# Causal mask of the second attention scores: added by TensorE instead of cut by GpSimd, with the exponentials taken twice from PSUM

## What is computed

```python
x = x + 0.5 * ffn(layernorm(x))      # silu(x Wg) * (x Wu), times Wd; hidden width 2048
x = x + attention(layernorm(x))      # 16 heads of 32
x = x + 0.5 * ffn(layernorm(x))

q, k = unit_norm(q), unit_norm(k)    # then rotary embedding on every other head
logits = einsum('bshd,bthd->bhst', q, k) * q_gain
logits = where(causal, logits, finfo.min)
attn   = softmax(logits, axis=-1)
y      = einsum('bhst,bthd->bshd', attn, v)
```

## Time and profile before

| | |
|---|---|
| profiled execution | 2897.56 us |
| its span | 2895.8 us |
| TensorE (PE) busy | 2765.8 us, 96% |
| VectorE (DVE) busy | 1773.8 us, 61% |
| ScalarE (ACT) busy | 1193.0 us, 41% |
| GpSimd (POOL) busy | 535.8 us, 19% |

### The profile page before, as it was taken

One profiled execution on the slowest core, in us unless ns is written; L12 is line 12 of the kernel. 1 busy time (PEld: TensorE's weight loads), 2 busy tenths in 40 slices (PEclk: granted clock), 3 DMA queues, 4 the chain that ended last, 5 costly groups with the idle time before them and its releaser, 6 DMA issues.

```text
span 2895.8 us, 56172 instructions
## 1 busy us (share of the span) xinstructions
PE 2765.8 (96%) x23232; PEld 2029.6 (70%) x23232; DVE 1773.8 (61%) x4156; ACT 1193.0 (41%) x2218; POOL 535.8 (19%) x820
## 2 busy tenths in 40 slices
PE   4699989999999999999999999999999999998899
PEld 4467666777767776777767777677767777676676
DVE  8655766656566565666656666565656656566643
ACT  5233544444433443344433445344433443445422
POOL 0103122112030311203012131212103030123100
PEclk8899999999999999999999999999999999999999
DMA  6000000000000000000000000000000000000000
GB/s 249 15 1 1 1 1 1 16 1 16 1 1 16 16 1 1 1 16 16 1 1 1 16 16 2 1 16 9 9 1 1 16 16 1 1 1 9 1 9 15
DMA packets 15486, 37.28 MB, mean 13 GB/s; under 512 B 1408, under 2 KB 1408, under 8 KB 14720
## 3 DMA queue, kind: packets, MB, share of 16 engines
q1 hardware_dynamic: 15232, 33.70, 3.2%
HBM read 25.31 MB, written 8.39 MB: 12 GB/s over the span
## 4 chain that ended last, share of the span: by engine, by line
PE 84%; DVE 10%; ACT 3%; issue 2%; POOL 1%; DMA 0%; SPq 0%; DVEq 0%; ACTq 0%
PE psum L906 24%; PE psum L908 24%; PE psum L907 24%; PE psum L1055 2%; PE psum L1032 2%; PE psum L1067 1%; DVE mneg L820 1%; PE psum L1014 1%; DVE arena L841 1%; PE psum L949 1%; PE psum L1010 1%; DVE arena L768 1%; DVE arena L770 1%; PE psum L1033 1%; DVE arena L763 1%
## 5 line engine op out<-in xcount | busy, mean ns | idle before, releaser
L906 PE MATMUL psum<-arena,WG 128*128 128x256 f16 x2048 | 559.9, 273 | 1.4 <-DVE arena L763 1.4
L908 PE MATMUL psum<-arena,WG 128*128 128x256 f16 x2048 | 559.8, 273 | 0.0
L907 PE MATMUL psum<-arena,WG 128*128 128x256 f16 x2048 | 559.6, 273 | 0.0
L906 PE MATMUL psum<-arena,WU 128*128 128x256 f16 x2048 | 559.1, 273 | 0.0
L908 PE MATMUL psum<-arena,WU 128*128 128x256 f16 x2048 | 558.8, 273 | 0.0
L907 PE MATMUL psum<-arena,WU 128*128 128x256 f16 x2048 | 558.8, 273 | 0.0
L768 DVE SCALAR_TENSOR_TENSOR arena<-arena,psum 128x256 f32<-128x256 f32 x512 | 214.8, 420 | 529.1 <-ACT arena L643 528.1
L643 ACT ACTIVATE arena<-psum,tscale 128x256 f32<-128x256 f32 x512 | 241.8, 472 | 671.8 <-PE psum L908 671.7
L906 PE MATMUL psum<-WD,arena 128*128 128x512 f16 x1024 | 388.6, 379 | 12.7 <-DVE arena L774 12.7
L908 PE MATMUL psum<-WD,arena 128*128 128x512 f16 x1024 | 388.5, 379 | 0.0
L907 PE MATMUL psum<-WD,arena 128*128 128x512 f16 x1024 | 388.4, 379 | 0.0
(11 more groups left out here) (139 smaller groups left out, 4543.1 us busy)
## 6 DMA issues: line engine op xcount, KB each, us to landing
arena<-in_L_attn_x SPq DMA_DIRECT2D x16, 512.0 KB, 3.6
out<-arena SPq DMA_DIRECT2D x16, 512.0 KB, 2.8
arena<-in_L_ffn_w_gate SPq DMA_DIRECT2D x4, 1024.0 KB, 9.2
arena<-in_L_ffn_w_up SPq DMA_DIRECT2D x4, 1024.0 KB, 8.3
WD<-in_L_ffn_w_down SPq DMA_DIRECT2D x4, 1024.0 KB, 10.6
arena<-in_L_attn_w_qkv SPq DMA_DIRECT2D x1, 3072.0 KB, 20.6
WQ<-in_L_attn_w_out SPq DMA_DIRECT2D x1, 1024.0 KB, 22.8
ropet<-rope_table SPq DMA_DIRECT2D x1, 128.0 KB, 2.1
```

What stands on the lines that cost most here:

```text
L906: T_.matmul(o, lhs(0), rhs(0), start=first, stop=False)
L907: T_.matmul(o, lhs(0), rhs(1), start=False, stop=False)
L908: return T_.matmul(o, lhs(1), rhs(0), start=False, stop=last)
```

## The change

- A second constant, `maskk`, is made on GpSimd at the start: MASKED (-1e36) below its diagonal and 0 elsewhere.
- In "scores" each of the four tiles gets a second matmul of `identb` and `maskk`, as "scores max" has it with `maskq`.
- GpSimd's stage "exp" is gone, with the semaphores `exp_done` and `cut_done`.
- "exp high" takes the exponential again, from the scores in PSUM to float16 `PHI`, where it copied `P32`. It waits for `pv_ps` alone now.
- TensorE overwrites banks 0 to 2 after `phi_done` of the scores in them, where it was after `exp_done`.

```diff
+    maskk = sb("maskk", P, BF16)
...
-            for m in (ident, ident16, identb, maskq):
+            for m in (ident, ident16, identb, maskq, maskk):
...
-            def exp(b, hf, h, m):
...
-                wait("exp_done", 2 * k + m + 1)
-                if m:
-                    zero(P32[:, KSEG[1]:KSEG[1] + P].unsqueeze(1), 1)
-                    zero(P32[:, KSEG[3]:KSEG[3] + 2 * P].rearrange("p (a n) -> p a n", a=2), 2).then_inc(s["cut_done"], 1)
-                else:
-                    zero(P32[:, 0:P].unsqueeze(1), 1).then_inc(s["cut_done"], 1)
...
             def exp_high(b, hf, h, m):
-                k, c = head_no(b, hf, h), PCOLS[m]
-                if hf or h:
+                k, c1, c = head_no(b, hf, h), hf * HH + h, PCOLS[m]
+                if c1:
                     wait("pv_ps", k)
-                wait("cut_done", 2 * k + m + 1)
-                nc.scalar.activation(PHI[:, c], P32[:, c], ACT.Copy).then_inc(s["phi_done"], 1)
+                nc.scalar.activation(PHI[:, c], ps(0, 0, SW)[:, c], ACT.Exp, bias=lnbias[:, 0:1],
+                                     scale=hscale[:, c1:c1 + 1]).then_inc(s["phi_done"], 1)
...
-                        ins = T_.matmul(ps(0, KSEG[t], w), KT[0:ST + MR, h, t * P:(t + 1) * P], QT[0:ST + MR, h, t * P:S], start=True, stop=True)
+                        T_.matmul(ps(0, KSEG[t], w), KT[0:ST + MR, h, t * P:(t + 1) * P], QT[0:ST + MR, h, t * P:S], start=True, stop=False)
+                        ins = T_.matmul(ps(0, KSEG[t], P), identb[:, :], maskk[:, :], start=False, stop=True)
                     if bank != 1:
                         ins.then_inc(s["s2_ps"], 1)
-                scored[0] = ("exp_done", k)
+                scored[0] = ("phi_done", k)
```

More of the change, by code:

```diff
@@ L174, in build @@
         st_hi st_lo qt_ps kt_ps qt_ev kt_ev s1_ps smax_done mst_done mt_ps mt_copied mrow_done
-        s2_ps exp_done cut_done phi_done plo_done pv_ps y_read ynorm_done yt_ps yt_hi yt_lo op_ps
+        s2_ps phi_done plo_done pv_ps y_read ynorm_done yt_ps yt_hi yt_lo op_ps
         gu_ps tanh_done a_done gated h_hi h_lo down_done dve_chain pool_chain"""
@@ L481, in _ @@
                                              base=0, pattern=[[-1, P]], channel_multiplier=1))
-            nc.gpsimd.affine_select(out=maskq[:, :], in_=maskq[:, :], compare_op=ALU.is_ge, fill=MASKED,
-                                    base=0, pattern=[[-1, P]], channel_multiplier=1).then_inc(s["c_made"], 1)
+            link(nc.gpsimd.affine_select(out=maskq[:, :], in_=maskq[:, :], compare_op=ALU.is_ge, fill=MASKED,
+                                         base=0, pattern=[[-1, P]], channel_multiplier=1))
+            nc.gpsimd.affine_select(out=maskk[:, :], in_=maskk[:, :], compare_op=ALU.is_ge, fill=MASKED,
+                                    base=0, pattern=[[1, P]], channel_multiplier=-1).then_inc(s["c_made"], 1)
             pool.wait_ge(s["gmax_in"], 1)
@@ L551, in pickers @@
                 wait("sel_done", 1)
-            run({"stats": stats, "qk out": qkv_out, "unit": rotate, "exp": exp, "scales": scales, "pickers": pickers})
+            run({"stats": stats, "qk out": qkv_out, "unit": rotate, "scales": scales, "pickers": pickers})
         @block.scalar
@@ L624, in exp @@
                     wait("plo_done", 2 * k - 1 + m)
-                nc.scalar.activation(P32[:, c], ps(0, 0, SW)[:, c], ACT.Exp, bias=lnbias[:, 0:1], scale=hscale[:, c1:c1 + 1]).then_inc(s["exp_done"], 1)
+                nc.scalar.activation(P32[:, c], ps(0, 0, SW)[:, c], ACT.Exp, bias=lnbias[:, 0:1], scale=hscale[:, c1:c1 + 1])
             def exp_high(b, hf, h, m):
-                k, c = head_no(b, hf, h), PCOLS[m]
-                if hf or h:
+                k, c1, c = head_no(b, hf, h), hf * HH + h, PCOLS[m]
+                if c1:
                     wait("pv_ps", k)
-                wait("cut_done", 2 * k + m + 1)
-                nc.scalar.activation(PHI[:, c], P32[:, c], ACT.Copy).then_inc(s["phi_done"], 1)
+                nc.scalar.activation(PHI[:, c], ps(0, 0, SW)[:, c], ACT.Exp, bias=lnbias[:, 0:1],
+                                     scale=hscale[:, c1:c1 + 1]).then_inc(s["phi_done"], 1)
             def y_turn(b, hf, g):
```

## The result

The changed kernel takes 2918.86 us (median of 4 executions, 2918.3 to 2919.75) against 2897.36 us for the kernel before on the same chip. The ratio is 1.0076, with a 95% interval of 1.0057 to 1.0093: it is slower. The kernel before has two groups of times on that chip, 2892.9 to 2895.2 us (12 executions, mean granted clock 0.989 or 0.990) and 2897.2 to 2899.0 us (9 executions, 0.987 or 0.988); of its four times beside the first result three are of the upper group, and so is the profiled one, 0.988, which accounts for 2.4 us of the gap between a difference of 21.5 us here and 25 us there. The profiled execution took 2919.15 us, its span 2917.4 us.

What follows compares the result with a forecast made beforehand. TensorE was taken to bound batches 1 to 6, the order of waits batches 0 and 7. Terms of 23.0 and 8.6 us, 31.6 on 2897.56, gave 2929.2, predicted as 2929 us; own range 2922 to 2936, wide 2914 to 2944.

Steps and rivals of the forecast that it cites:

- the rival with free thin batches: In batches 0 and 7, stalls fall where TensorE would have waited anyway: 2920.6 us; chance 0.12, shared with a small gain.
- my sum: Whole kernel: 23.0 us in batches 1 to 6 plus 8.6 in batches 0 and 7, on the profiled 2897.56: 2929.2 us.
- Mask matmuls in the middle: TensorE, batches 1 to 6: 96 heads at 0.24 us, 60 ns per mask matmul, paid in full: 23.0 us.
- Exposed weight loads: TensorE: each mask costs a 98 ns load of `identb`, 37.6 us in batches 1 to 6; 2946.2 us, chance 0.03.
- Second exponential: ScalarE's "exp high" as Exp from PSUM: 777 and 984 ns, 38.8 us more work, beside TensorE's stream in batches 1 to 6.
- The cut counted at nothing: GpSimd's zeroing between "exp" and "exp high" goes; longer exponentials take back the gain to 0.1 us; counted at nothing.
- Held banks in the middle: Banks 0 to 2, batches 1 to 6: tightest place has 1.48 us, needs 0.30 and 0.07, so no wait.
- the thin batches' 8.6 us: Batches 0 and 7: half of 17.2 us is paid, from 7.7 for masks and 9.5 for stalls on held banks.
- The stalls: TensorE waiting for held banks in batches 0 and 7: 20 of 31 places fall short, 9.5 us in all, half paid.
- A further stretch of clock: Each further stretch at the 1.2 GHz level in batches 0 and 7 costs about 1.5 us; two with full payment make 2941.
- Theory B: From the experiments: in batches 0 and 7 there are real prices and a real gain, which cancel.
- Theory A: From the experiments: masks in batches 1 to 6 are the price, and all the rest is worth nothing.

## Why the prediction was right, and where it was off

The direction, what bounds the kernel and the wide range held: 2918.9 us lies in 2914 to 2944. It lies outside the forecast's own 2922 to 2936, and the rival with free thin batches (2920.6) came nearer than the 2929 I named. That is luck for the rival: masks in the thin batches are not free. The executions compared differ by 10.0 us from my sum, 2919.15 against 2929.2, of which 2.7 (an estimate) are the two stretches at 1.2 GHz that only the kernel before has, 1.5 the earlier start, and 5.7 a term that I had too large.

- Mask matmuls in the middle, 23.0 us forecast from two groups of the trace: 22.97 measured, and gone to 0.1 us when the masks are left out. The Trainium skill's figure of about 81 ns per pair ("TensorE: Matmul & The Clock Gate", "Back-to-back issue gap") does not hold here: 60 ns, and 56 for a second one, so the measurement decides. Exposed weight loads are excluded with it.
- Second exponential 777 and 984 ns: 774 and 983 measured. That it costs nothing in the middle: right. That it costs nothing in the thin batches: wrong, 1.45 us in batch 0.
- The cut counted at nothing because the exponential takes back what it gives: the net was close, but both terms are real, -2.6 and +1.45 us in batch 0. The way from the second "exp" to the end of the second "exp high" that I had at 2.55 us is 442.25 to 444.78, 2.53 us, in the changed kernel.
- Held banks in the middle: no wait, right.
- The term that was mis-sized is the thin batches' 8.6 us, half of 7.7 for masks and half of 9.5 for stalls on the held banks. Measured are 0.8 us in batch 0 and an estimated 2.1 in batch 7, 2.9 in all. The masks' half was right. The stalls were wrong twice: recorded are 3.3 us in 12 places, not 9.5 in 20, and the hold added 0.1 to 0.3 us to batch 0 where half of the stalls would be over 2. I had added 0.30 us for two longer exponentials to ends that the missing hop moves forward, having worked out that very balance a paragraph earlier. And a share of the chain did not tell what a stall costs.
- For batch 0 the sum is -2.6 (cut) + 1.8 (masks) + 0.1 (hold) + 1.45 (exponential) = +0.8 us. The same traces give batch 7, from its first scores to the end, with 1.37 us taken off for each stretch at 1.2 GHz (an estimate: two in the kernel before, one each with the high part copied, none in the others): -2.3 + 2.1 + 0.2 + 2.1 = +2.1 us. In another order of steps the masks cost less: 1.35 us in batch 0 and an estimated 1.1 in batch 7 when they are left out of the changed kernel.
- A further stretch of clock, which I had at about 1.5 us, cost 1.37.
- Theory B stands for the thin batches in kind, though a part of it, that stalls are paid, fell for stalls as short as the change's. Theory A stands for the middle.

## What to carry to other kernels

Split the span by what limits it before weighing a change: here 23.0 us came out of the stretch where one engine is full, and elsewhere terms of one to three microseconds nearly cancelled. A second trace, or the clock over the same stretches, tells what of the rest is not the change's: here some 4 us. When a hop goes, move the starts behind it before adding longer instructions to them. And ask of a stall whose work it delays: the same bank hold was nearly free to the end of "exp high", and cost 68 us one stage later.

## What the runs showed of the hardware that was not expected

A mask matmul that alternates with matmuls of 104 rows costs 60 ns and one that follows another mask 56 ns. In the kernel before, float16 matmuls show the same 4 ns behind a change from 104 to 128 rows (113 against 109 ns), while a change of the stationary matrix at the same height shows none. An Exp from PSUM with float16 output takes as long as with float32 (774 and 777 ns at 512 columns). One stretch at 1.2 GHz, in a batch where TensorE had been idle for part of the time before, cost 1.37 us, and of two traces with the same program in that batch one had it and the other did not.
